# Refining delta in PSUM: ScalarE evacuates the residuals, VectorE forms only the step, v is transposed into its bank

## What is computed

```python
q, k, v = silu(conv(x @ W)), per head; q and k l2-normalized
def step(S, inp):
    qt, kt, vt, gt, bt = inp
    S = S * jnp.exp(gt)[..., None]
    err = jnp.einsum('bhk,bhkv->bhv', kt, S)
    delta = bt[..., None] * (vt - err)
    S = S + kt[..., None] * delta[:, :, None, :]
    ot = jnp.einsum('bhk,bhkv->bhv', qt, S)
    return (S, ot)
```

## Time and profile before

| | |
|---|---|
| runs | 6806.0 us median of 3 (6805.97 to 6807.41) |
| span of the profiled execution | 6807.0 us; no time of its own outside the span is given for it |
| PE, busy share of the span | 92% |
| PEld | 64% |
| DVE | 77% |
| ACT | 40% |
| POOL | 26% |

### The profile page before, as it was taken

The page is one execution under the profiler, slowest core; times in us unless marked ns, Lnnn a source line. Parts: engine busy times, 40 slices in busy tenths (PEclk is TensorE's granted clock), DMA queues, the critical chain, the costliest instruction groups (busy, mean ns, idle before and its releaser), DMA issues. The chain is left out here.

```text
span 6807.0 us, 109951 instructions
## 1 busy us (share of the span) xinstructions
PE 6239.8 (92%) x33784; PEld 4326.8 (64%) x33784; DVE 5260.2 (77%) x8850; ACT 2728.7 (40%) x4746; POOL 1756.5 (26%) x1580
## 2 busy tenths in 40 slices
PE   6799999999999999999999999999999999799998
PEld 2476666666666666666666667666666667534433
DVE  7788888888888888888888888888888888211111
ACT  2344444444444444444444444444444444101000
POOL 1233323333232333332323333323333333000000
PEclk7899999999999999999999999999999999799999
DMA  1100000000000000000000000000000000112111
GB/s 62 30 18 26 18 26 17 24 17 26 18 25 19 26 16 24 18 25 19 25 19 25 16 17 25 19 26 19 25 19 25 16 18 18 68 67 80 59 69 52
DMA packets 183441, 197.62 MB, mean 29 GB/s; under 512 B 25000, under 2 KB 128040, under 8 KB 179120
## 3 DMA queue, kind: packets, MB, share of 16 engines
q1 hardware_dynamic: 111024, 152.84, 7.1%
q10 hardware_dynamic: 72192, 41.95, 1.9%
HBM read 150.45 MB, written 44.30 MB: 29 GB/s over the span
## 5 line engine op out<-in xcount | busy, mean ns | idle before, releaser
L620 PE MATMUL bank<-xT,weights 128*128 (+1 forms) x4096 | 2173.4, 628 | 76.8 <-ACT gate L1046 30.9
L1145 POOL TENSOR_TENSOR KR<-KR,total 128x256 f32<-128x256 f32 x768 | 759.8, 989 | 1716.8 <-PE bank L646 1716.8
L646 PEld LDWEIGHTS bank<-KQ,KR 128*128 128x128 f32 x7168 | 916.2, 191 | 249.5 <-issue 212.5
L857 DVE SCALAR_TENSOR_TENSOR conv<-pre,taps,conv 128x512 f32<-128x512 f32 x1152 | 981.6, 852 | 27.3
L646 PE MATMUL bank<-KQ,KR 128*128 128x128 f32 x7168 | 952.8, 275 | 2.9 <-DVE total L874 2.9
L620 PEld LDWEIGHTS bank<-xT,weights 128*128 128x128 f32 x4096 | 657.5, 193 | 287.6 <-issue 214.8
L872 DVE TENSOR_TENSOR KQ<-KQ,total 128x512 f32<-128x512 f32 x768 | 549.7, 716 | 320.9 <-PE bank L646 303.9
L892 DVE COPY_PREDICATED all_pairs<-level_mask,bank 128x512 f32<-128x512 int32 x896 | 785.7, 877 | 0.0
L668 PEld LDWEIGHTS bank<-T_inv,pairs 128*128 128x128 f32 x3072 | 456.0, 192 | 467.3 <-issue 219.3
L668 PE MATMUL bank<-T_inv,pairs 128*128 128x64 f32 x3072 | 654.2, 338 | 61.0 <-DVE T_inv L908 59.4
L874 DVE TENSOR_TENSOR total<-total 128x128 f32<-128x128 f32 (+5 forms) x768 | 581.7, 757 | 0.0
(11 more groups left out here) (166 smaller groups left out, 9847.2 us busy)
## 6 DMA issues: line engine op xcount, KB each, us to landing
beta_u<-beta_scratch SPq DMA_DIRECT2D x128, 256.0 KB
decay_u<-decay_scratch SPq DMA_DIRECT2D x128, 256.0 KB
y_scratch<-y_out ACTq DMA_DIRECT2D x128, 256.0 KB, 2.3
y_in<-y_scratch SPq DMA_DIRECT2D x32, 1024.0 KB, 4.8
xt<-in_L_attn_hidden_states SPq DMA_DIRECT2D x8, 1024.0 KB, 5.2
x_in<-in_L_attn_hidden_states SPq DMA_DIRECT2D x32, 256.0 KB, 4.9
out<-o_out ACTq DMA_DIRECT2D x32, 256.0 KB, 2.0
w<-in_L_ffn_W SPq DMA_DIRECT2D x8, 704.0 KB, 4.7
```

The lines of the kernel that those rows point to most:

```text
L620: last = nc.tensor.matmul(bank[w % 2][:], weights[par][:, w, k, :], xT[:, k, bass.ds(j * UC, UC)], start=k == 0, stop=k == KC - 1)
L646: last = nc.tensor.matmul(to[:, :, i], KR[:, cols(i)], halves(KQ[:, :, cols(i)], l, 1), start=True, stop=True)
L857: nc.vector.scalar_tensor_tensor(conv[:, w], pre[:, w, :, t:t + P], taps[par][:, w, t:t + 1], conv[:, w], ALU.mult, ALU.add).then_inc(step ...
L1145: nc.gpsimd.tensor_tensor(first_halves, first_halves, second.to_broadcast([P, UC >> (l + 1), 1 << l]), ALU.mult).then_inc(keys_scaled.sem, 1)
```

## The change

Bank 7 keeps U and takes the products of the refinement on top of it; bank 5 keeps X U and takes the corrections on top. So the residual is bank 7 itself, and ACT copies it out (twice per unit, new `take_residual` on ACT); delta after the first correction isn't formed in SBUF: DVE forms only the step, bank 5 minus the first delta, and `refine(1)` multiplies that step into bank 7. After the second correction ACT copies bank 5 to `delta`. The plain copy of U goes. The product by which v enters bank 7 becomes four transposes, ahead of the state products instead of between them. On PE `correct_by_residual(1)` now stands ahead of `sums(1)`. On ACT the Silu of k and its Square are parted by `take_residual(0)`, `take_residual(1)` stands ahead of `inverse_norm(0)`, and the copy of delta between `inverse_norm(0)` and `inverse_norm(1)`.

```diff
             def apply_inverse(to, first):
                 for i in range(B):
-                    last = nc.tensor.matmul(bank[5][:, cols(i)], X[:, cols(i)], to[:, cols(i)], start=True, stop=True)
+                    last = nc.tensor.matmul(bank[5][:, cols(i)], X[:, cols(i)], to[:, cols(i)], start=first and i == 0,
+                                            stop=True, skip_group_check=True)
...
                 if n == 0:
-                    wait(pe, u_kept, b, 1)
                     wait(pe, pairs_kept, b, 1)
                     wait(pe, delta_ready, b, 1)
                 else:
-                    wait(pe, delta_refined, b, n)
+                    wait(pe, step_ready, b, n)
+                by = delta if n == 0 else step_delta
                 for i in range(B):
-                    last = nc.tensor.matmul(bank[7][:, cols(i)], pairs_scan[:, 0, cols(i)], delta[:, cols(i)], start=True,
-                                            stop=True)
+                    last = nc.tensor.matmul(bank[7][:, cols(i)], pairs_scan[:, 0, cols(i)], by[:, cols(i)], start=False,
+                                            stop=True, skip_group_check=True)
...
                 for i in range(B):
-                    nc.tensor.matmul(bank[7][:, cols(i)], v_u[:, cols(i)], ident[:], start=True, stop=False)
+                    nc.tensor.matmul(bank[7][:, cols(i)], v_u[:, cols(i)], ident[:], is_transpose=True, start=i == 0,
+                                     stop=False, skip_group_check=True)
+                for i in range(B):
                     last = nc.tensor.matmul(bank[7][:, cols(i)], KQ_scan[:, 0, cols(i)], state[:, cols(i)], start=False,
...
             refine(1)
+            correct_by_residual(1)
             sums(1)
-            correct_by_residual(1)
             project(3, (3,))
             if b is not None:
-                wait(pe, delta_refined, b, REFINEMENTS)
+                wait(pe, delta_refined, b, 1)
...
# DVE
-                nc.vector.tensor_tensor(residual[:], bank[7][:], U_sb[:], ALU.add).then_inc(residual_ready.sem, 1)
...
+            def delta_step(n):
                 wait(dve, correction_done, b, n + 1)
-                if n >= 1:
-                    wait(dve, delta_refined, b, n)
-                nc.vector.tensor_tensor(delta[:], delta[:], bank[5][:], ALU.add).then_inc(delta_refined.sem, 1)
+                wait(dve, delta_ready, b, 1)
+                nc.vector.tensor_tensor(step_delta[:], bank[5][:], delta[:], ALU.subtract).then_inc(step_ready.sem, 1)
...
-            take_residual(0)
             scale(LEVELS - 1)
-            correct_delta(0)
+            delta_step(0)
             keep_pairs(LEVELS - 1)
-            take_residual(1)
-            correct_delta(1)
             convolve(2, range(2, TAPS))
# ACT
+            def take_residual(n):
+                wait(act, product_done, b, n + 1)
+                nc.scalar.activation(residual[:], bank[7][:], ACT.Copy).then_inc(residual_ready.sem, 1)
...
                 nc.scalar.activation(U_r[:], bank[7][:], ACT.Copy).then_inc(u_ready.sem, 1)
-                nc.scalar.activation(U_sb[:], bank[7][:], ACT.Copy).then_inc(u_kept.sem, 1)
...
-            silu_squares(1)
+            take_silu(1)
+            take_residual(0)
+            take_squares(1)
             nc.scalar.preload_act_table_set("natural_log_exp_and_others")
+            take_residual(1)
             inverse_norm(0)
+            if b is not None:
+                wait(act, correction_done, b, REFINEMENTS)
+                nc.scalar.activation(delta[:], bank[5][:], ACT.Copy).then_inc(delta_refined.sem, 1)
             inverse_norm(1)
```

More of the change, by code:

```diff
@@ L419, in attention @@
     chunk_decay = sb("chunk_decay", [P, B])
-    U_sb = sb("U_sb", [P, UC])
+    step_delta = sb("step_delta", [P, UC])
     U_r = sb("U_r", [P, UC], F32R)
@@ L458, in attention @@
     chunk_decay_ready = signal("chunk_decay_ready", 1)
-    residual_ready = signal("residual_ready", REFINEMENTS)
-    delta_refined = signal("delta_refined", REFINEMENTS)
+    step_ready = signal("step_ready", REFINEMENTS - 1)
     hats_ready = signal("hats_ready", 1)
@@ L485, in attention @@
     u_ready = signal("u_ready", 1)
-    u_kept = signal("u_kept", 1)
     delta_ready = signal("delta_ready", 1)
+    residual_ready = signal("residual_ready", REFINEMENTS)
+    delta_refined = signal("delta_refined", 1)
     y_sq_ready = signal("y_sq_ready", 1)
@@ L704, in sums, with apply_inverse @@
                                  stop=True).then_inc(sums_done.sem, 1)
-            def apply_inverse(to):
+            def apply_inverse(to, first):
                 for i in range(B):
-                    last = nc.tensor.matmul(bank[5][:, cols(i)], X[:, cols(i)], to[:, cols(i)], start=True, stop=True)
+                    last = nc.tensor.matmul(bank[5][:, cols(i)], X[:, cols(i)], to[:, cols(i)], start=first and i == 0,
+                                            stop=True, skip_group_check=True)
                 return last
@@ L730, in correct_by_residual @@
                 wait(pe, residual_ready, b, n + 1)
-                apply_inverse(residual).then_inc(correction_done.sem, 1)
+                apply_inverse(residual, False).then_inc(correction_done.sem, 1)
             project(0, range(KC))
@@ L781, in step @@
                 wait(pe, u_ready, b, 1)
-                apply_inverse(U_r).then_inc(delta_done.sem, 1)
+                apply_inverse(U_r, True).then_inc(delta_done.sem, 1)
             sums(0)
@@ L916, in add_identity_to_z @@
                                         halves(ident_each[:], l, 0), ALU.add).then_inc(zi_ready.sem, 1)
[L918 to L924, removed]
-                nc.vector.tensor_tensor(residual[:], bank[7][:], U_sb[:], ALU.add).then_inc(residual_ready.sem, 1)
-            def correct_delta(n):
+            def delta_step(n):
                 if b is None:
@@ L1020, in take_projection, with take_silu @@
                                      ACT.Copy).then_inc(ready.sem, 1)
-            def silu_squares(w):
+            def take_silu(w):
                 if a is None:
@@ L1029, in silu_squares, with take_squares @@
                                      ACT.Silu).then_inc(silu_ready.sem, 1)
+            def take_squares(w):
+                if a is None:
+                    return
                 wait(act, silu_ready, a, w + 1)
@@ L1072, in take_x @@
                                      ACT.Copy).then_inc(x_ready.sem, 1)
+            def take_residual(n):
+                if b is None:
+                    return
+                wait(act, product_done, b, n + 1)
+                nc.scalar.activation(residual[:], bank[7][:], ACT.Copy).then_inc(residual_ready.sem, 1)
             silu_gate()
@@ L1085, in step @@
             take_x(4)
-            silu_squares(0)
+            take_silu(0)
+            take_squares(0)
             take_t(5)
```

## The result

The changed kernel takes 6890.7 us (median, 6889.3 to 6893.0), the kernel before 6806.7 beside it: a ratio of 1.0123, interval 1.0109 to 1.0137, 84 us slower. The prediction was 6844, in a range up to 6882. The direction was right, the size was not: the time lies above the range.

A forecast was written before the change was run, and what follows sets the result against it. Bound: the chain of releases PE, DVE, PE at the step's seam, not a busy share. Second refinement +0.59 us a step, its start 0.26 earlier; 0.30 taken, 126 x 0.30 = 38 us, 6844 us; range 6710 to 6882.

The forecast's parts named there:

- relief of DVE counts in full: Rival: three DVE instructions of 0.69 us a step saved in full, 261 us, giving 6545; chance 0.03.
- v by transposes: Four PE transposes replace eight fp32 instructions: 0.45 us saved, only 0.12 us of it left for PE's own line.
- the lock: DVE and POOL exclude each other at level 6; POOL stays first by 0.19 us, the four-column L874 still slow.
- D: Start of delta_step(0) on DVE, after level 6: predicted at 24.82 for 25.08, 0.26 us earlier.
- The faster rival: L874 gets the ports before POOL at level 6: L795 0.74 us earlier, 93 us less, 6713; chance 0.18.
- the second refinement: From delta_step(0) to the output product: 4.11 us becomes 4.70, +0.59, sums(1) waiting for ACT's Ln behind the correction.
- v by a transpose: Prediction's step on v entering bank 7; also held the clock stays 1.00, transposes costing it nothing by the trace.
- The slower rival: Transposes save nothing that lasts, D stays 25.08, full +0.59 us a step paid: 74 us, 6880; chance 0.12.

The follow-up runs named there:

- both orders put back: Changed kernel with sums(1) again ahead of correct_by_residual(1) on PE and inverse_norm(0) ahead of take_residual(1) on ACT: 6755.4 us, 0.9919 of the kernel before.
- the small product is made to go first: DVE's four-column product (total) put ahead of its large one at level 6: 6645.0 us on the changed kernel with orders put back, 6677.7 on the kernel before.
- filling the second gap with unread work: Changed kernel plus two unread 512-column PE products between refine(1) and correct_by_residual(1): 6833.5 us, 1.0035 of the kernel before.
- the early gate: Changed kernel with both PE and ACT orders put back, project(3, (3,)) moved ahead of refine(1): 6756.4 us, 0.9923 of the kernel before.
- the filler ahead of refine(1): Changed kernel plus two unread 512-column PE products issued ahead of refine(1): 6868.8 us, 1.0086 of the kernel before.

## Why the prediction was right and wrong

**Right: what bounds the step.** The chain of releases does, not a busy share. Of the rival that relief of DVE counts in full nothing came true: 2.1 us a step less work on DVE, and the step longer. Even with both orders put back it was worth 0.2 us a step (43.56 with the transposes alone, 43.37).

**Right: v by transposes.** 0.12 us on PE's line and 0.14 at the lock; alone it makes the kernel before 32 us faster.

**Right: the lock.** POOL kept its lead, with 0.21 us (3275.43 against 3275.64; 0.19 predicted), and L877 took 1.22 us. D came 3.81 us after refine(0), 3.82 predicted. The faster rival did not come about, but its price for D was right: where the small product is made to go first, D moves by the 1.07 us. (The 22.17 that the prediction gives ACT's first residual is 0.02 short of its own sum, 21.00 + 1.19; the trace has 1.17. Nothing hangs on it.)

**Right in kind, small in size: the second refinement.** 4.65 us for 4.70. With 0.05 less there, 0.01 at D and 0.10 us more given back between the output product and the state update, an undisturbed step grew by 0.17 us, where the sum had 0.33 and 0.30 was taken: 22 us instead of 38. This term alone would have been well inside the range.

**Wrong: the clock.** The failed step is the one in "v by a transpose" that took the granted clock of 1.00 as a property of the kernel and let it change nothing. The prediction asked of the clock only what the transposes would do to it. It saw that sums(1) used to lie in PE's wait and would lie behind the correction, and it priced the length of the chain by that, but not that the wait was then empty at both ends: 1.16 and 0.69 us idle with only the eight instructions of refine(1) between. The clock then fell there 42 times, where the kernel before has no fall (58 low steps for 8), and that cost 85 - 22 = 63 us; filling the second gap with unread work gave back 57 of them. The slower rival (6880) was near the measured time by its number, not by its reason: nothing was lost of what the transposes save.

The Trainium skill (TensorE: Matmul & The Clock Gate, Part 1) says that an idle PE has its clock throttled to half, and that activity releases it. The rows of the low step agree, 0.50 of the granted clock, though no single gap there is longer than 1.16 us and the kernel before had gaps of 1.01 and 0.32 around the same products at a clock of 1.00. What the Trainium skill (TensorE: Matmul & The Clock Gate, Part 4) says of transposes, that they do not count as busy time in the same way, is not borne out here as a cost: the kernel before with eight transposes a step has 7 low steps, and the changed kernel without the new ones 39.

Open is why the idle time behind refine(1) weighs more than that ahead of it (the early gate moved idle time elsewhere and the clock held, the filler ahead of refine(1) did not hold it), and why the low steps come in the order in which they come.

## What to carry to other kernels

Before moving work out of an engine's wait, ask what else that work did there: on PE even two unread products, which took 0.47 of 0.69 us of idle time, held the clock, and a move that lengthened the chain by 0.2 us cost three times that much again. Read the granted clock step by step and not as a mean of the run (0.979 and 0.969 looked alike), count its falls and where in the step they begin, and sort the steps by it before explaining a difference in length. Where an instruction on a few columns takes 1.2 us, look at who holds its ports: exchanging two independent instructions was worth 110 to 131 us here, twice what the change is worth with its orders put back.

## What was not expected of the hardware

Part-time throttling: with 1.16 and 0.69 us idle around refine(1), PE's clock fell in some steps and held in others with the same timeline (full clock in the step shown from 3275, half in the next, whose rows up to 3323.3 are the same to 0.02 us). And a lock between DVE and POOL that is settled by starts 0.01 to 0.2 us apart, at a price of 0.5 to 1.1 us for the loser (0.68 to 1.23 and 0.61 to 1.21 above, 0.16 to 1.22 for the small product).
